# Ten idle products on TensorE ahead of the last stage of a graph network kernel

## The reference

```
h = relu(layernorm(x))
e = relu(concat(h[dst], edge_attr) @ W1.T + b1)      # a row of 128 per edge
e = relu(e @ W2.T + b2)
agg = segment_sum(e, src) / max(count(src), 1)       # a row of 128 per node
z = relu(concat(h, agg, u[0]) @ Wa.T + ba)
out = x + z @ Wb.T + bb                              # 64 per node
```

## Time and profile before

| | us |
|---|---|
| median of 3 runs | 1896.42 |
| lowest, highest | 1895.69, 1898.47 |
| the profiled execution | 1902.48 |
| its span, first to last instruction | 1900.7 |
| TensorE busy (matrix instructions) | 1732.0 (91%) |
| GpSimd busy | 1509.7 (79%) |
| ScalarE busy | 1428.0 (75%) |
| VectorE busy | 1340.0 (71%) |
| mean granted clock of TensorE | 0.972 |

### The profile page before, as it was taken

One profiled execution on the slowest core, in us unless ns is written; L12 is line 12 of the kernel. 1 busy time (PEld: TensorE's weight loads), 2 busy tenths in 40 slices (PEclk: granted clock), 3 DMA queues, 4 the chain that ended last, 5 costly groups with the idle time before them and its releaser, 6 DMA issues.

```text
span 1900.7 us, 43131 instructions
## 1 busy us (share of the span) xinstructions
PE 1732.0 (91%) x12376; PEld 1463.0 (77%) x12376; DVE 1340.0 (71%) x4868; ACT 1428.0 (75%) x2591; POOL 1509.7 (79%) x991
## 2 busy tenths in 40 slices
PE   5898888999999999999899999999999999976828
PEld 3676777888888888888788888888888888866725
DVE  8665655777777777778677777777777777755727
ACT  4687877888888888888788888888888888842315
POOL 8488888888888888888888888888888888878850
PEclk9999999999999999999999999999999999988968
DMA  9988888999999999999899999999999999997755
GB/s 330 269 169 145 156 148 141 199 197 205 195 207 187 199 203 199 194 205 197 176 199 194 199 202 200 195 194 209 202 191 201 200 204 202 199 210 155 159 136 198
DMA packets 312201, 369.10 MB, mean 194 GB/s; under 512 B 40832, under 2 KB 196064, under 8 KB 311328
## 3 DMA queue, kind: packets, MB, share of 16 engines
q1 hardware_dynamic: 175200, 302.12, 55.1%
q0 software_dynamic: 135360, 62.15, 34.5%
q10 hardware_dynamic: 1408, 2.03, 0.3%
HBM read 203.87 MB, written 159.27 MB: 191 GB/s over the span
## 4 chain that ended last, share of the span: by engine, by line
POOL 53%; issue 20%; DMA 11%; PE 9%; ACT 3%; DVE 2%; SPq 1%; POOLq 0%; ACTq 0%; DVEq 0%
POOL sums L819 48%; DMA sums<-regA,idx 9%; POOL sums L807 5%; PE bank L1351 2%; PE bank L1400 2%; PE bank L1362 1%; DMA sums<-vscat,vidx 1%; PE bank L1374 1%; ACT h L921 1%; PE bank L1390 1%; ACT regA L929 1%; PE bank L1276 1%; PE bank L1476 1%; ACT regA L955 0%; DMA p_table<-regB 0%
## 5 line engine op out<-in xcount | busy, mean ns | idle before, releaser
L819 POOL DMA_INDIRECT sums<-regA,idx x844 | 1318.3, 1562 | 293.0 <-issue 242.6
L1351 PEld LDWEIGHTS bank<-h,regC 128*128 128x128 f32 x3072 | 387.4, 193 | 180.7 <-ACT h L940 127.8
L1351 PE MATMUL bank<-h,regC 128*128 128x130 f32 x3072 | 432.0, 284 | 64.5 <-ACT h L940 64.5
L1374 PE MATMUL bank<-regA,L 128*128 128x512 f32 x806 | 432.3, 619 | 2.8 <-DVE regA L1143 2.7
L1400 PE MATMUL bank<-w,h 128*128 128x128 f32 x3224 | 430.1, 277 | 0.0
L1400 PEld LDWEIGHTS bank<-w,h 128*128 128x128 f32 x3224 | 396.8, 194 | 1.1 <-ACT h L921 0.6
L921 ACT ACTIVATE h<-bank,b1c 128x512 f32<-128x512 f32 x403 | 275.6, 684 | 136.9 <-PE bank L1374 131.9
L1362 PE MATMUL bank<-regC 128*128 128x129 f32 x2352 | 296.9, 280 | 23.0 <-DVE regB L1130 12.7
L1390 PEld LDWEIGHTS bank<-h,regC 128*128 128x128 f32 x1688 | 218.9, 191 | 119.7 <-issue 91.3
L1362 PEld LDWEIGHTS bank<-regC 128*128 128x128 f32 x2352 | 277.4, 194 | 37.3 <-ACT vscat L961 21.9
L904 ACT ACTIVATE regC<-bank 128x520 f32<-128x520 f32 x384 | 231.8, 604 | 87.8 <-PE bank L1351 84.5
(11 more groups left out here) (143 smaller groups left out, 1526.9 us busy)
## 6 DMA issues: line engine op xcount, KB each, us to landing
regC<-slots SPq DMA_DIRECT2D x294, 260.0 KB, 5.6
regA<-in_ea SPq DMA_DIRECT2D x202, 256.0 KB
slots<-regC SPq DMA_DIRECT2D x192, 260.0 KB
src<-rows_src SPq DMA_DIRECT2D x107, 256.0 KB
slots<-regC SPq DMA_DIRECT2D x192, 138.1 KB
sums<-regA,idx POOLq DMA_INDIRECT x844
dstR<-rows_dst SPq DMA_DIRECT2D x101, 128.0 KB
sums<-zeros SPq DMA_DIRECT2D x20, 645.0 KB, 6.7
```

The lines of the kernel that those rows point to most:

```text
L819: nc.gpsimd.indirect_dma_start(out=sums[k], out_offset=bass.IndirectOffsetOnAxis(ap=idx[:, n % RING, t:t + 1], axis=0), in_=scat[:, n % 4, ...
L1351: last = T.matmul(psSlot(t)[:, k, :], place, h2[:, g % 2, t, :], start=True, stop=True)
L1374: T.matmul(psL1(s % 2), L[:, s % RING, :], R[:, s % RING, :], start=True, stop=True).then_inc(l1_done, 1)
```

## The change

Between the h rows of the first four chunks and the loop over the chunks, TensorE gets ten products of `ident` with 512 columns of `zeros`, written to bank 4, whose content nobody reads: three at once, four after all scatters have landed, three after the loads of chunk 0 have landed. Nothing else is changed.

```diff
--- before.py
+++ after.py
@@ -1459,6 +1459,17 @@
             pe.wait_ge(acc_ready, len(UNIT_NO))
             for n in range(ZLEAD):
                 z_of_h(n)
+
+            def idle_products(n):
+                for _ in range(n):
+                    T.matmul(bank[:, 4, :], ident[:, :], zeros[:, 0:GE], start=True, stop=True)
+
+            idle_products(3)
+            for k in range(NSETS):
+                pe.wait_ge(added[k], 16 * SCATTERS[k])
+            idle_products(4)
+            pe.wait_ge(acc_in[0], 16 * NSETS)
+            idle_products(3)
             for c in range(NCH + 2):
                 if c < NCH:
                     pe.wait_ge(agg_ready, c + 1)
```

## The result

The changed kernel takes 1901.84 us (median of 22 runs, 1896.69 to 1906.09), the kernel before 1897.74 (22 runs beside them, 1895.38 to 1903.27). The medians are 4.1 us apart, the means (1901.42 and 1898.46) 3.0. The ratio measured is 1.0016, with a 95% interval of 1.0009 to 1.0023: **3.0 us slower**, 1.7 to 4.4. The forecast was no change, 1896.3 us with a range up to 1898.8; both the time and the sign were missed.

What follows compares the result with a forecast made beforehand. The last stage was taken to rest mostly on VectorE, slowed in one stretch by TensorE at half clock, at most 4.70 us. The sum 0 + 0 + 0 - 0.1 against the 1896.42 us median gave 1896.3 us, range 1893.8 to 1898.8.

Steps and rivals of the forecast that it cites:

- Nothing is removed or moved: Whole kernel: TensorE only gains ten products and five waits; other queues issue what they did, no DMA added.
- the 0.1 us gained: Last stage: chunk 2's means start up to 0.2 us sooner, carried to the end; taken as 0.1 us.
- hidden, price nothing: After the h rows: three products, 0.86 to 1.71 us each, end in TensorE's 26.07 us hole before the scatters land.
- The next four and the last three: Behind the scatters and chunk 0's load: clock rises within the four; all end between 1845.8 and 1847.2, hidden.
- The third rival: Products behind the scatters: zeros do not lift the clock, chunk 1's means come 2.1 us later; 1898.5 us, chance 0.08.
- my way to slower: Behind the scatters: seven products at half level end at 1850.07 and delay chunk 0's transposes 2.38 us; the third rival.
- The 0.46 us of chunk 0's transposes: Chunk 0: transposes take 0.66 us in place of 1.12, but the 0.46 us is lost waiting for VectorE; price nothing.
- The fall between the chunks: Chunks 0 to 2: TensorE idles 2.70 and 3.0 us, so the clock falls around 1851 or at latest in the second.
- All eleven: Trace of before: every TensorE idle time at full level lasting 2.6 us or longer goes with a clock fall.
- The first rival: Chunks 3 to 5: the clock stays up and up to 4.70 us go; 1891.7 us, chance 0.10.
- The second rival: Last stage: the clock's fall shifts its next rise, TensorE saves 1.6 us; 1894.8 us, chance 0.09.
- The bound of 0.2%: Whole kernel: about 0.2%, 3.8 us, is what a measurement can tell from no change; the same had chance 0.82.

Runs made afterwards that it cites:

- after: The changed kernel itself, its first trace: ten idle products against the kernel before; 1901.84 us, ratio 1.0016.
- after2: The changed kernel once more, unchanged, for a second trace; ratio 1.0012 to the kernel before.
- small10: The changed kernel with one column in place of 512 in each of the ten products; ratio 1.0017 to the kernel before.
- bridge: The changed kernel plus five products of 512 columns, two behind chunk 0's transposes and three behind chunk 0's product; ratio 0.9998 to the kernel before.
- pad64: The kernel before plus 64 one-column products right after the h rows, without waits; ratio 0.9994 to the kernel before.
- first10: The changed kernel with ten products in place of three ahead of the waits, four and three still behind them; ratio 1.0013 to the kernel before.
- onewait: The changed kernel with one wait, for the fourth table's scatters, in place of the waits for all four; ratio 1.0001 to the kernel before.
- lean2: lean once more, unchanged; ratio 1.0000 to the kernel before.
- bridge1: bridge with one wait, for the fourth table's scatters, in place of the waits for all four; ratio 1.0005 to the kernel before.
- lean: bridge1 without the first three products, those after the h rows; ratio 0.9996 to the kernel before.

## Why the prediction was wrong

The step that failed is the first sentence of the part-by-part account: "Nothing is removed or moved", with "no DMA is added" behind it. TensorE's own instructions come by DMA. Inserting some 45 moved a transfer from the h rows to the first loads: chunk 0 came 1.3 to 1.5 us late and chunk 2 0.8 us late, in both traces of the change. In one of the two the last transfer met the load of chunk 10 as well, for 2.0 us. Neither was a term of the sum, which had nothing but the 0.1 us gained. How the 3.0 us of the runs divide between the two, the traces don't settle.

Point by point:

- **The first three products, "hidden, price nothing".** Their time is hidden. With the four waits behind them they belong to what moves the transfer: it came at the first loads in all four traces with exactly three full or one-column products ahead of four waits (after, after2, small10, bridge), 1.2 to 1.5 us after the landing that ends these waits, and stayed beside the h rows in all others. pad64, far longer, got an extra one. Whether the waits hold the transfer back, or a few instructions more or less suffice, no run tells.
- **The next four and the last three.** Right: the clock rose in them, 6.1 us after their start, the end of the 3.1 to 6.1 that was foretold. All seven took 9.31 us, against 7.7 to 9.1 foretold (1838.1 to between 1845.8 and 1847.2); that their end at 1846.5 lies in that stretch is luck, since the scatters landed 1.0 us earlier. The third rival, zeros that don't lift the clock, falls. So my way to slower was the wrong mechanism: the waits and products did sit where they were foretold, and it was the fetching of them that cost.
- **The 0.46 us of chunk 0's transposes.** Right in kind: 0.66 us, ended at 1848.82, and chunk 1's means still wait for VectorE.
- **The fall between the chunks.** Right: in the changed kernel's traces and in first10 and onewait it fell between chunks 0 and 1, and the gain was given back. The argument was weaker than it looked. "All eleven" idle times from 2.6 us up went with a fall, but here one of 2.34 us did, while in after2 one of 2.92 us (ahead of 1888.10) and in lean2 one of 3.22 us (ahead of 908.18) did not. The Trainium skill, TensorE: Matmul & The Clock Gate, section "Part 4: PE-mode transpose", says that transposes don't count for the clock as products do. The fall here agrees with it: from the last idle product to chunk 0's agg product lie 5.6 us with nothing but transposes. bridge puts products in there and keeps the clock, but it shortens the idle times too, so no run isolates it.
- **The first rival, up to 4.7 us if the clock stays up.** bridge shows its mechanism and its size in the two steps: 11.90 - 7.64 = 4.3 us against the trace on which the prediction was made. The mean of the three traces of before is 9.81, so there are only 2.2 us to win on average; one trace was taken for the kernel. What is open is why the runs show not even those: bridge1 and lean have the shortest last stages (58.9 and 58.7 us), yet ratios of 1.0005 and 0.9996. The last scatter's landing varies from 1833.4 to 1841.9 between traces, more than the gain, and whether something ahead of it takes the gain back wasn't found.
- **The second rival, a shifted rise.** The rise comes 26.7 and 23.1 us after the landing in the two traces of the change, 27.0, 22.4 and 15.9 us in the three of before. It differs more between executions of one kernel than between the kernels, so nothing can be said for or against this rival.
- **The bound of 0.2%.** The loss of 0.16% is under the line that the prediction drew, but 22 runs of each kernel put it outside no change. Of the 5.5 us by which the median missed the forecast, 1.3 are the kernel before itself: three runs of it gave 1896.42, 22 gave 1897.74.

## What to carry to other kernels

An engine's instructions are traffic too: before inserting some ahead of a stage that waits on loads, look in the table of DMA queues for instruction transfers and ask where the next one will fall. The cheap test is the same instructions with no work in them (one column), and the same number elsewhere. And take a stretch's cost from several executions when it hangs on the clock: here the prize was 4.3 us by one trace and 2.2 us by three.

## What the runs showed of the hardware

- A single 16 KB instruction transfer, 1.1 to 1.8 us long, delays loads already issued: chunk 0 by 1.3 to 1.9 us (after 6.61, after2 6.39, small10 7.00, bridge 6.63, against a mean of 5.1 for the three traces of before). Its loads were all issued before the transfer began, so the stalled issue isn't what made them late. The delays are near the transfers' own lengths (1.10, 1.26, 1.83, 1.69), as if one DMA engine were held and the load not whole without its share; no row tells the engine. The Trainium skill, DMA: Bandwidth & Descriptors, section "Queues, rings and completion order", says that each engine alternates between queues by whole packets, which would do this.
- The same transfer stalls the issue of a load on two queues at once, SP's 1.64 and ScalarE's 1.62 us, in place of 0.43 to 0.64 in the three traces of before.
- Where the late transfer falls differs between executions of one program: 1880.99 and 1873.35 in the two traces of the change, 5.6 and 0.4 us after the first issue for chunk 10, with steps of 4.31 and 6.18 us; 1886.08, 1875.68 and 1873.06 in those of before, 10.1, 5.8 and 5.8 us after it, with steps of 3.63, 4.35 and 4.40. Why it differs stays open.
